# A cross-attention kernel: its first rows on two DMA queues, its key weights split later on ScalarE

## The chip, the cores and the metric

The program runs on one core of a Trainium2 chip. The metric is the time of one execution in device microseconds (us). The engines are TensorE (PE, with its weight loads PEld), VectorE (DVE), ScalarE (ACT), GpSimd (POOL) and SyncE (SP). SP and ACT also issue the DMAs, each on a queue of its own.

## The reference

One row block `x` of 256 tokens by 512 reads a context of 25088 tokens by 512. Three blocks follow one another: cross-attention with a sigmoid instead of a softmax, causal attention with latents, and a layer of eight experts of which each token takes one. The change touches only what stands at the start of the first:

```
def ref_xattn(q, ctx):                       # q = layernorm(x)
    qp = q @ Wq.T + bq                       # 256 x 128
    kp = ctx @ Wk.T + bk                     # 25088 x 128
    vp = ctx @ Wv.T + bv
    z = sigmoid(qp @ kp.T / sqrt(128))
    return z @ vp
x = x + ref_xattn(layernorm(x), ctx_1024)
x = x + attn(layernorm(x)); x = x + ffn(layernorm(x))
```

## The kernel before

Products that need more precision than one pass gives are made of three: each operand is split into a rounded "high" part (a Copy on ACT) and a "low" part (a subtraction on DVE), and high x high, high x low and low x high are summed in PSUM. The context goes by in 49 tiles of 512 tokens. For each tile `b` the kernel computes its keys (L336), the scores against the queries (L354), the sigmoid (L364) and the sum of weights times context rows (L395). The value projection is applied once, after the loop. A context tile comes in twice, turned (`rawt`, split into `th`, `tl`) and plain (`rawn`, split into `nh`, `nl`), in halves of 512 KB.

No scheduler decides the order. `put` appends an operation to a list of its engine, with the semaphores that it waits for, and each engine plays its list in the order in which the program wrote it. An engine that waits holds up all that stands behind it on its list. DMAs are issued in the same way, as an entry on the list of SP ("sync") or of ACT ("scalar").

The head of the program does this:

- L189 loads the two halves of `x` (128 rows each, 256 KB) into `x_s`, both on SP's queue. Then SP issues the two halves of the first turned context tile (`rawt`), the query weights (`zf`), and more of the context. ACT's queue has the key weights `wk_s` (256 KB, L190), the identity matrix `id_s` (64 KB, used to transpose) and the biases `bqk_s` (1 KB).
- L267 lets PE multiply zeros (`wz`) 22 times, so that it works while the first data are on their way.
- L272 runs a Sqrt on one element, which loads that table early. L273 writes `wkh`, the high part of the key weights.
- L281 and L282 (DVE) take mean and variance of each half of `x`, the first half and then the second. L283, called the root here, takes the square root on ACT. L284 to L289 make the reciprocal deviation of it on DVE with one Newton step. L296 writes the normalised rows `h_s`, and L299 transposes them on PE into PSUM.
- L304 runs a Sigmoid on one element of ACT, for which the table of the main loop is loaded. Behind it ACT splits the turned context (`th`, L230), copies the transposed rows to `hT` (L318), and goes on with `nh`, `qph` and `kph`.
- L292 (`first_keys`) is the keys of tile 0, in an order of its own: high parts of the first two chunks, their product with `wkl` (the low part of the key weights, L307 on DVE), and so on. L322 is the queries. Then come the first scores, L354.

```
root = put("scalar", lambda e: e.activation(stat(18), mv[:, :, 1], ACT.Sqrt, bias=eps_s[:]), [m, EPS0], "lnq")
...
put("scalar", lambda e: e.activation(sq[0:1, 6:7], sq[0:1, 0:1], ACT.Sigmoid), [SQ0], "sgw")
low_t = [split_t(0, k) for k in range(2)]
```

Of the kernel before, what the change touches and what calls it, by code (L numbers as in the profile page):

```python
# [6 lines left out]
ACT = mybir.ActivationFunctionType  # L7
# [13 lines left out]
class Queues:  # L21
# [8 lines left out]
    def put(self, eng, fn, waits=(), sig=None, inc=1):  # L30
        for m in waits:
            sem, value = m
            if self.seen.get((eng, sem), 0) < value:
                self.seen[(eng, sem)] = value
                self.lists[eng].append(("wait", self.sems[sem], value))
        if sig is None:
            self.lists[eng].append(("do", fn, None, 0))
            return None
        if sig not in self.sems:
            self.sems[sig] = self.ctx.enter_context(self.nc.semaphore("s_" + sig))  # L40
            self.count[sig] = 0
        self.count[sig] += inc
        self.lists[eng].append(("do", fn, self.sems[sig], inc))
        return sig, self.count[sig]

    def dma(self, eng, dst, src, sig, waits=()):
        return self.put(eng, lambda e: e.dma_start(dst, src), waits, sig, 16)
# [11 lines left out]
def program(nc, x, ctxn, ctxt, wkt, wqt, wvt, bqk, bv, kvd, kup, vup, wq, qrope, krope, wo, gate, wg, wu, wd,  # L59
# [3 lines left out]
    with ExitStack() as ctx:  # L63
        q = Queues(nc, ctx)
        put, dma = q.put, q.dma

        def sb(name, shape, dt=F32):
            return ctx.enter_context(nc.sbuf_tensor(name, shape, dt))
# [11 lines left out]
        def bank(i):  # L80
            return ps[i // 2][:, 512 * (i % 2):512 * (i % 2) + 512]
# [4 lines left out]
        x_s = sb("x_s", [P, 2, D])  # L86
# [42 lines left out]
        def sm(name, shape, dt=F32):  # L129
            return stream.enter_context(nc.sbuf_tensor(name, shape, dt))  # L130
# [12 lines left out]
        wk_s = sm("wk_s", [P, 512])  # L143
        wkh = sm("wkh", [P, 512], F32R)
# [41 lines left out]

        xr = x.rearrange("a (r p) d -> p (a r) d", p=P)

        DX = [dma("sync", x_s[:, r, :], xr[:, r, :], f"dx{r}") for r in range(2)]  # L189
        DWK = dma("scalar", wk_s[:], wkt, "dwk")  # L190
        DID = dma("scalar", id_s[:], ident, "did")
        wq0 = zf
# [20 lines left out]
        def load_n(b, k):  # L213
            old = [] if b == 0 else hm if (b, k) == (1, 1) else n_rd[0, 1] if (b, k) == (2, 1) else n_rd[b - 1, k]
            n_ld[b, k] = dma("sync", raw_n(b, k), ctn[b][:, HALF[k]], "dn1b" if (b, k) == (1, 1) else f"dn{k}", old)
# [11 lines left out]
        def split_t(b, k):  # L227
            n = HALF[k]
            free = [] if b == 0 else [KW[k], Tl[0, k]] if b == 1 else [KP[b - 1]]
            Th[b, k] = put("scalar", lambda e: e.activation(th[:, n], raw_t(b)[:, n], ACT.Copy), [t_ld[b, k], *free], "th")  # L230
            return lambda: split_tl(b, k)
# [31 lines left out]
            return low if later else low()  # L263

        WZ = put("gpsimd", lambda e: e.memset(wz[:], 0.0), (), "wz")
        for k in range(22):
            put("tensor", lambda e: e.matmul(bank(7), wz[:, 0:P], wz[:], start=True, stop=True), [WZ])  # L267
        Z0 = put("gpsimd", lambda e: e.memset(zacc[:], 0.0), (), "pz")
        ONE = put("gpsimd", lambda e: e.memset(one_s[:], 1.0), (), "pz")
        EPS0 = put("vector", lambda e: e.memset(eps_s[:], EPS), (), "eps")  # L270
        SQ0 = put("vector", lambda e: e.memset(sq[:], 1.0), (), "sq0")
        WARM = [put("scalar", lambda e: e.activation(sq[0:1, 1:2], sq[0:1, 0:1], ACT.Sqrt), [SQ0], "lnw")]  # L272
        WKH = put("scalar", lambda e: e.activation(wkh[:], wk_s[:], ACT.Copy), [DWK], "wkh")  # L273

        def stat(k, n=2):
            return st[:, k:k + n]
# [3 lines left out]
        for r in range(2):  # L280
            m = put("vector", lambda e, r=r: e.bn_stats(st[:, 6 * r:6 * r + 6], x_s[:, r, :]), [DX[r]], "ln")  # L281
            m = put("vector", lambda e, r=r: e.bn_aggr(mv[:, r, :], st[:, 6 * r:6 * r + 6]), [m], "ln")  # L282
# [7 lines left out]
        def first_keys(w, t, c, wait, opens=False, mark=None):  # L290
            n = slice(512 * c, 512 * c + 512)
            return put("tensor", lambda e: e.matmul(bank(0), w[:, c * P:(c + 1) * P], t[:, n], start=opens,  # L292
                                                    stop=mark == "kp"), wait, mark)

        def first_rows(r):
            h = put("vector", lambda e: e.tensor_scalar(h_s[:, r, :], x_s[:, r, :], mv[:, r, 0:1], stat(26 + r, 1),  # L296
                                                        ALU.subtract, ALU.mult), [m], "lnh")
            for k in range(4):
                f = put("tensor", lambda e, k=k: e.transpose(bank(6 + r)[:, k * P:(k + 1) * P],  # L299
                                                             h_s[:, r, k * P:(k + 1) * P], id_s[:]),  # L300
                        [h, DID], "lnt" if k == 3 else None)
            return f

        put("scalar", lambda e: e.activation(sq[0:1, 6:7], sq[0:1, 0:1], ACT.Sigmoid), [SQ0], "sgw")  # L304
        low_t = [split_t(0, k) for k in range(2)]
        hm = [first_rows(r) for r in range(2)]
        WK = put("vector", lambda e: e.tensor_tensor(wkl[:], wk_s[:], wkh[:], ALU.subtract), [WKH], "wkl")  # L307
        load_n(1, 1)
        low_t[0]()
        for k in range(2):  # L310
            for c in (2 * k, 2 * k + 1):
                first_keys(wkh, th, c, [WKH, Th[0, k]], opens=c == 0)
            for c in (2 * k, 2 * k + 1):
# [17 lines left out]
        def keys(b, turns=None):  # L331
            for i, c in turns or [(i, c) for i in range(3) for c in range(4)]:
                w, t = [(wkh, th), (wkl, th), (wkh, tl)][i]
                old = [KPL[b - 2]] if b >= 2 and i == 0 else []
                wait = old + [WKH, WK, Tl[b, c // 2] if i == 2 else Th[b, c // 2]]
                KP[b] = put("tensor", lambda e, w=w, t=t, c=c, i=i: e.matmul(  # L336
# [347 lines left out]
        f = add()  # L684
# [91 lines left out]
        def a_sums(qt):  # L776
            m = put("vector", lambda e: e.reciprocal(einv[:, qt, :], esum[:, qt, :]),
                    [EX[p, u] for p in range(NU) if units[p][0] == qt for u in range(2)], "rc")
            return put("vector", lambda e: e.tensor_copy(
                eexp, einv[:, qt, :].rearrange("p (h o) -> p h o", o=1).to_broadcast([P, 16, 32])),  # L780
                [m] + ([RR[0]] if qt else []), "rc")

        def a_spread(qt, bk, wait):
            for t in range(4):
                f = put("tensor", lambda e, t=t: e.matmul(
                    bank(bk)[:, P * t:P * t + P], eexp[:, 4 * t:4 * t + 4, :].rearrange("p h o -> p (h o)"), id_s[:],
                    start=(t == 0), stop=(t == 3)), wait, "rr" if t == 3 else None)
            return f
# [68 lines left out]
        f = a_sums(0)  # L857
# [20 lines left out]
        f = a_sums(1)  # L878
# [4 lines left out]
        f = a_spread(1, 4, [f, EX[4, 0]])  # L883
# [221 lines left out]
```

How the kernel before makes its waits and increments, by code:

```python
    def play(self, eng, e):  # L49
        for item in self.lists[eng]:
            if item[0] == "wait":
                e.wait_ge(item[1], item[2])
            else:
                ins = item[1](e)
                if item[2] is not None:
                    ins.then_inc(item[2], item[3])
```

## Time and profile before

| | us |
|---|---|
| median of 3 runs | 577.13 (576.76 to 577.57) |
| the profiled execution | 577.08 |
| its span, from first to last instruction | 575.3 |
| outside the span | 1.8 |
| PE busy | 569.4 |
| DVE busy | 456.4 |
| ACT busy | 401.7 |

The span begins when the first engine works. What the profile calls idle is time before an instruction in which its engine had nothing to do, with the releaser behind the arrow.

### The profile page before, as it was taken

What the parts mean: (1) busy time and instruction counts of PE and PEld (TensorE: products, weight loads), DVE (VectorE), ACT (ScalarE), POOL (GpSimd) and SP (SyncE); (2) the same over time, 40 slices, a digit from 0 to 9 for tenths busy, and PEclk for the clock granted to TensorE, in tenths of its full rate; (3) what the DMA queues carried; (4) which work ended last, traced back from release to release, by engine and by line L of the source; (5) the groups of instructions that cost most, each with busy time, mean ns of one, the idle gap of its engine ahead of it and who ended that gap; (6) DMA issues with size and microseconds to landing.
All of it is one profiled execution on the core that took longest, in us unless ns stands there. A gap on an engine that the chain in (4) does not pass through costs nothing.

```text
span 575.3 us, 8075 instructions
## 1 busy us (share of the span) xinstructions
PE 569.4 (99%) x3010; PEld 477.2 (83%) x3010; DVE 456.4 (79%) x494; ACT 401.7 (70%) x542; POOL 1.7 (0%) x7
## 2 busy tenths in 40 slices
PE   8999999999999999999999999999999999999998
PEld 5888888888888888888888888888888887877887
DVE  6987878787878797889787978787878798887742
ACT  6776767676768687768667877776776784797321
POOL 1000000000000000000000000000000000000000
DMA  8668777768677877777778877767787743000201
GB/s 327 229 199 248 233 237 236 225 221 240 218 220 251 265 244 238 236 255 259 226 246 254 254 227 250 219 221 222 217 275 234 229 142 114 33 1 2 74 1 38
DMA packets 33239, 115.90 MB, mean 201 GB/s; under 512 B 4080, under 2 KB 4784, under 8 KB 32944
## 3 DMA queue, kind: packets, MB, share of 16 engines
q1 hardware_dynamic: 32768, 115.05, 62.7%
q8 instruction: 24, 0.39, 0.3%
q10 hardware_dynamic: 432, 0.33, 0.2%
q14 instruction: 15, 0.12, 0.1%
HBM read 114.84 MB, written 0.52 MB: 201 GB/s over the span
## 4 chain that ended last, share of the span: by engine, by line
PE 92%; ACT 3%; DMA 2%; DVE 2%; issue 1%; DVEq 0%; ACTq 0%; SPq 0%
PE ps L395 44%; PE ps L336 22%; PE ps L354 12%; PE ps L924 4%; PE ps L956 2%; DMA rawn<-in_ctxn 1%; PE ps L813 1%; PE ps L525 1%; ACT w L742 1%; PE ps L722 1%; PE ps L657 1%; PE ps L749 1%; PE ps L606 1%; DMA x_s<-in_x 1%; PE ps L292 1%
## 5 line engine op out<-in xcount | busy, mean ns | idle before, releaser
L395 PE MATMUL ps<-nh,zl 128*128 128x512 f32 x388 | 142.8, 390 | 0.1
L395 PE MATMUL ps<-nh,zh 128*128 128x512 f32 x388 | 142.7, 390 | 0.0
L395 PE MATMUL ps<-nl,zh 128*128 128x512 f32 x388 | 142.5, 389 | 0.0
L369 DVE TENSOR_TENSOR zl<-zf,zh 128x1024 fp32r<-128x1024 f32 x49 | 60.1, 1226 | 79.6 <-ACT zh L368 79.6
L255 DVE TENSOR_TENSOR nl<-rawn,nh 128x1024 fp32r<-128x1024 f32 x96 | 114.0, 1221 | 1.4 <-issue 0.8
L235 DVE TENSOR_TENSOR tl<-rawt,th 128x1024 fp32r<-128x1024 f32 x96 | 113.2, 1218 | 1.8 <-ACT th L230 1.7
L252 ACT ACTIVATE nh<-rawn 128x1024 fp32r<-128x1024 f32 x96 | 99.8, 1057 | 12.3 <-DMA rawn<-in_ctxn 11.1
L230 ACT ACTIVATE th<-rawt 128x1024 fp32r<-128x1024 f32 x96 | 96.3, 1053 | 2.3 <-DMA rawt<-in_ctxt 2.3
L364 ACT ACTIVATE zf<-ps 128x512 f32<-128x512 f32 x98 | 58.2, 597 | 56.3 <-PE ps L354 50.6
L395 PEld LDWEIGHTS ps<-nh,zl 128*128 128x128 f32 x388 | 72.7, 188 | 16.0 <-DVE zl L369 1.0
L395 PEld LDWEIGHTS ps<-nl,zh 128*128 128x128 f32 x388 | 72.9, 188 | 15.2
L395 PEld LDWEIGHTS ps<-nh,zh 128*128 128x128 f32 x388 | 72.5, 188 | 15.5 <-ACT zh L368 0.5
L341 ACT ACTIVATE kph<-ps,bqk_s 128x512 fp32r<-128x512 f32 x49 | 33.8, 690 | 47.8 <-PE ps L336 47.7
L372 DVE TENSOR_TENSOR zacc<-zacc,zf 128x1024 f32<-128x1024 f32 x49 | 59.8, 1220 | 0.0
L354 PE MATMUL ps<-qph,kpl 128*128 128x256 f32 x196 | 55.0, 283 | 0.0
L354 PE MATMUL ps<-qpl,kph 128*128 128x256 f32 x196 | 55.0, 283 | 0.0
L354 PE MATMUL ps<-qph,kph 128*128 128x256 f32 x196 | 54.8, 282 | 0.0
L368 ACT ACTIVATE zh<-zf 128x1024 fp32r<-128x1024 f32 x49 | 52.1, 1063 | 1.6
L336 PE MATMUL ps<-th,wkh 128*128 128x512 f32 x192 | 52.6, 394 | 0.0
L336 PE MATMUL ps<-th,wkl 128*128 128x512 f32 x192 | 51.7, 390 | 0.0
L336 PE MATMUL ps<-tl,wkh 128*128 128x512 f32 x192 | 51.6, 390 | 0.0
L336 PEld LDWEIGHTS ps<-th,wkl 128*128 128x128 f32 x192 | 36.1, 188 | 8.1
(193 smaller groups left out, 618.5 us busy)
## 6 DMA issues: line engine op xcount, KB each, us to landing
rawn<-in_ctxn SPq DMA_DIRECT2D x97, 512.0 KB, 6.4
rawt<-in_ctxt SPq DMA_DIRECT2D x96, 512.0 KB, 4.8
h_s<-in_wg SPq DMA_DIRECT2D x4, 512.0 KB, 6.7
h_s<-in_wu SPq DMA_DIRECT2D x4, 512.0 KB, 6.6
wds<-in_wd SPq DMA_DIRECT2D x4, 512.0 KB, 3.9
raw<-in_ctxt SPq DMA_DIRECT2D x2, 512.0 KB, 8.7
h_s<-in_wvt SPq DMA_DIRECT2D x2, 512.0 KB, 7.6
wq_s<-in_wq SPq DMA_DIRECT2D x1, 1024.0 KB, 10.1
```

The costliest lines, as they stand in the source:

```text
L230: Th[b, k] = put("scalar", lambda e: e.activation(th[:, n], raw_t(b)[:, n], ACT.Copy), [t_ld[b, k], *free], "th")
L235: Tl[b, k] = put("vector", lambda e: e.tensor_tensor(tl[:, n], raw_t(b)[:, n], th[:, n], ALU.subtract), [t_ld[b, k], Th[b, k]] + ([KL[k]] ...
L252: Nh[b, k] = put("scalar", lambda e: e.activation(hi, raw_n(b, k), ACT.Copy), [n_ld[b, k]] + free, "nh")
L255: Nl[b, k] = put("vector", lambda e: e.tensor_tensor(lo, raw_n(b, k), hi, ALU.subtract), [n_ld[b, k], Nh[b, k]] + free, "nl")
L336: KP[b] = put("tensor", lambda e, w=w, t=t, c=c, i=i: e.matmul(bank(b % 2), w[:, c * P:(c + 1) * P], t[:, c * 512:(c + 1) * 512], start=(i ...
L341: KPH[b] = put("scalar", lambda e: e.activation(kph[:], bank(b % 2), ACT.Identity, bias=bqk_s[:, 1:2]), [KP[b], DBK] + ([S[b - 1]] if b el ...
L354: m = put("tensor", lambda e, o=o, js=js, k=k, w=w, i=i, j=j: e.matmul(o, k[:, js], w[:], start=(i == 0 and j % 2 == 0), stop=(i == 2 and ...
L364: m = put("scalar", lambda e, g=g, gs=gs: e.activation(zf[:, gs], bank(2 + g), ACT.Sigmoid, scale=SC), [S[b, g]] + ([ZL[b - 1], ZA[b - 1]] ...
L368: ZH[b] = put("scalar", lambda e: e.activation(zh[b % 2][:], zf[:], ACT.Copy), [ZF[b]] + av, "zh")
L369: ZL[b] = put("vector", lambda e: e.tensor_tensor(zl[b % 2][:], zf[:], zh[b % 2][:], ALU.subtract), [ZH[b]] + av, "zl")
L372: ZA[b] = put("vector", lambda e: e.tensor_tensor(zacc[:], zacc[:], zf[:], ALU.add), [ZF[b], Z0] + ([ZA[b - 1]] if b else []), "za")
L395: m = put("tensor", lambda e, z=z, n=n, i=i, j=j, r=r: e.matmul(bank(4 + r), z[:, j * T + r * P:j * T + r * P + P], n, start=(b == 0 and i ...
```

## The change

The first half of `x` is issued on ACT's queue, ahead of the key weights, and the second half stays alone on SP's queue. The split of the key weights (`wkh`) is moved on ACT's list from before the root to behind it, which is ahead of the Sigmoid. The multiplications of zeros go from 22 to 20.

```
-        DX = [dma("sync", x_s[:, r, :], xr[:, r, :], f"dx{r}") for r in range(2)]
+        DX = [dma(("scalar", "sync")[r], x_s[:, r, :], xr[:, r, :], f"dx{r}") for r in range(2)]
         DWK = dma("scalar", wk_s[:], wkt, "dwk")
         DID = dma("scalar", id_s[:], ident, "did")
...
-        for k in range(22):
+        for k in range(20):
             put("tensor", lambda e: e.matmul(bank(7), wz[:, 0:P], wz[:], start=True, stop=True), [WZ])
...
-        WKH = put("scalar", lambda e: e.activation(wkh[:], wk_s[:], ACT.Copy), [DWK], "wkh")
...
+        WKH = put("scalar", lambda e: e.activation(wkh[:], wk_s[:], ACT.Copy), [DWK], "wkh")
         put("scalar", lambda e: e.activation(sq[0:1, 6:7], sq[0:1, 0:1], ACT.Sigmoid), [SQ0], "sgw")
```

ACT's list from the start of the program, of the kernel before (`x_s` is missing here, and L273 is the high part of the key weights, L283 the root):

```order
L47 DMA wk_s<-in_wkt 128x512
L47 DMA id_s<-in_ident 128x128
L47 DMA bqk_s<-in_bqk 128x2
L272 ACT_TABLE_LOAD
L272 ACTIVATE sq<-sq 1x1
L273 ACTIVATE wkh<-wk_s 128x512
L283 ACTIVATE st<-st,eps_s 128x2
L304 ACT_TABLE_LOAD
L304 ACTIVATE sq<-sq 1x1
L230 ACTIVATE th<-rawt 128x1024 x2
```

The same list of the changed kernel, in which L282 is the root and L303 the high part of the key weights:

```order
L47 DMA x_s<-in_x 128x512
L47 DMA wk_s<-in_wkt 128x512
L47 DMA id_s<-in_ident 128x128
L47 DMA bqk_s<-in_bqk 128x2
L272 ACT_TABLE_LOAD
L272 ACTIVATE sq<-sq 1x1
L282 ACTIVATE st<-st,eps_s 128x2
L303 ACTIVATE wkh<-wk_s 128x512
L304 ACT_TABLE_LOAD
L304 ACTIVATE sq<-sq 1x1
L230 ACTIVATE th<-rawt 128x1024 x2
```

One DMA is added at the head of ACT's queue, and `wkh` now stands between the root and the second table load.

SP's list at the same place, as a difference (`x_s` is the rows, `rawt` the turned context, `zf` holds the query weights):

```order
 L1024 UNCONDITIONAL_BRANCH
-L47 DMA x_s<-in_x 128x512 x2
+L47 DMA x_s<-in_x 128x512
 L47 DMA rawt<-in_ctxt 128x1024 x2
 L47 DMA zf<-in_wqt 128x512
```

SP issues one DMA less, so that all behind it moves up by one place; nothing else on SP's list, on DVE's or on PE's moves, but for the two multiplications of zeros.

## Rows read from the trace of the kernel before

**Rows 1.** One stretch: length, busy us (count) of PE, PEld, DVE, ACT, POOL, granted clock, DMA.

```profile
30.00:545.00 515.00, 513.09 (x2727) 433.14 (x2726) 420.55 (x440) 373.09 (x504) 0.00 (x0) 1.00 0.66 208
```

**Rows 2.** Chain that ended last, first 14 us: start, duration, what.

```profile
0.73 3.54 DMA x_s<-in_x
...
7.83 1.11 PE ps L299 x8
...
9.01 2.54 PE ps L292 x10
```

**Rows 3.** Timeline of ACT: start, duration, instruction, count, idle time before.

```profile
4.49 0.63 ACT L273 ACTIVATE wkh<-wk_s 128x512 fp32r<-128x512 f32 x1 [0.86 <-DMA wk_s<-in_wkt]
6.11 0.29 ACT L283 ACTIVATE st<-st,eps_s 128x2 f32<-128x2 f32 x1 [0.99 <-DVE st L282]
6.42 1.28 ACT L304 ACT_TABLE_LOAD   x1
...
7.82 1.99 ACT L230 ACTIVATE th<-rawt 128x1024 fp32r<-128x1024 f32 x2
...
13.78 0.69 ACT L341 ACTIVATE kph<-ps,bqk_s 128x512 fp32r<-128x512 f32 x1
```

**Rows 4.** Timeline of DVE, 4 to 10 us.

```profile
4.30 0.69 DVE L281 BATCH_NORM_STATS2 st<-x_s 128x6 f32<-128x512 f32 x1 [3.41 <-DMA x_s<-in_x]
5.03 0.18 DVE L282 BATCH_NORM_AGGREGATE st<-st 128x2 f32<-128x6 f32 x1
5.16 0.69 DVE L281 BATCH_NORM_STATS2 st<-x_s 128x6 f32<-128x512 f32 x1
...
8.15 0.68 DVE L307 TENSOR_TENSOR wkl<-wk_s,wkh 128x512 fp32r<-128x512 f32 x1
```

**Rows 5.** Timeline of DMA issues on both queues (SPq, ACTq).

```profile
0.73 0.86 SPq L47 DMA_DIRECT2D x_s<-in_x  x2
1.65 0.90 SPq L47 DMA_DIRECT2D rawt<-in_ctxt  x2
1.17 0.46 ACTq L47 DMA_DIRECT2D id_s<-in_ident  x1
```

**Rows 6.** DMAs issued 0.7 to 1.1 and 1.6 to 2.0 us: KB, us to landing.

```profile
wk_s<-in_wkt ACTq DMA_DIRECT2D x1, 256.0 KB, 3.7
x_s<-in_x SPq DMA_DIRECT2D x1, 256.0 KB, 3.5
...
rawt<-in_ctxt SPq DMA_DIRECT2D x1, 512.0 KB, 5.7
id_s<-in_ident ACTq DMA_DIRECT2D x1, 64.0 KB, 4.2
```

**Rows 7.** DMA packets, 2.8 to 3.6 us, then 5.2 to 6.4: packets, MB, share (q1 SP's, q10 ACT's).

```profile
DMA packets 160, 0.33 MB, mean 410 GB/s; under 512 B 0, under 2 KB 0, under 8 KB 160
q1 hardware_dynamic: 80, 0.16, 52.8%
q10 hardware_dynamic: 80, 0.16, 52.5%
...
DMA packets 208, 0.38 MB, mean 315 GB/s; under 512 B 116, under 2 KB 116, under 8 KB 208
```

**Rows 8.** The multiplications of zeros, L267 alone, in two stretches of 3 us: PE, PEld, clock.

```profile
1.30:4.30 3.00, 2.99 (x8) 1.06 (x9) 1.00 0.68 235
4.60:7.60 3.00, 3.00 (x15) 1.25 (x13) 1.00 1.03 378
```

**Rows 9.** Weight loads of PE that waited: idle time before and its releaser.

```profile
7.83 0.88 PEld L299 LDWEIGHTS ps<-id_s,h_s 128*128 128x128 f32 x8 [0.56 <-DVE h_s L296]
8.98 0.30 PEld L292 LDWEIGHTS ps<-th,wkh 128*128 128x128 f32 x2 [0.27 <-issue]
14.52 0.54 PEld L354 LDWEIGHTS ps<-qph,kph 128*128 128x128 f32 x4 [0.29 <-ACT kph L341]
```

**Rows 10.** Timeline of PE around its longest idle time behind the head.

```profile
488.27 0.71 PE L590 MATMUL ps<-id_s,h_s 128*128 128x128 f32 x4 [0.47 <-ACT h_s L586]
```

More of the change, by code:

```diff
@@ L187, in program @@
         xr = x.rearrange("a (r p) d -> p (a r) d", p=P)
-        DX = [dma("sync", x_s[:, r, :], xr[:, r, :], f"dx{r}") for r in range(2)]
+        DX = [dma(("scalar", "sync")[r], x_s[:, r, :], xr[:, r, :], f"dx{r}") for r in range(2)]
         DWK = dma("scalar", wk_s[:], wkt, "dwk")
@@ L265, in program @@
         WZ = put("gpsimd", lambda e: e.memset(wz[:], 0.0), (), "wz")
-        for k in range(22):
+        for k in range(20):
             put("tensor", lambda e: e.matmul(bank(7), wz[:, 0:P], wz[:], start=True, stop=True), [WZ])
@@ L272, in program @@
         WARM = [put("scalar", lambda e: e.activation(sq[0:1, 1:2], sq[0:1, 0:1], ACT.Sqrt), [SQ0], "lnw")]
-        WKH = put("scalar", lambda e: e.activation(wkh[:], wk_s[:], ACT.Copy), [DWK], "wkh")
         def stat(k, n=2):
@@ L302, in first_rows @@
             return f
+        WKH = put("scalar", lambda e: e.activation(wkh[:], wk_s[:], ACT.Copy), [DWK], "wkh")
         put("scalar", lambda e: e.activation(sq[0:1, 6:7], sq[0:1, 0:1], ACT.Sigmoid), [SQ0], "sgw")
```

## The prediction

> **What bounds the kernel now.** I read the stretches first. Between 30 and 545 us TensorE is busy for 513.09 of 515.00 us [rows 1]: the main loop is bound by PE, and it has next to no idle time in which a late start could be made up. So the question is only when PE begins its real work, and whether its chain from there stays as it is. The chain of waits says what sets that start: the first half of `x` (0.73 to 4.27 us), then the statistics and the root, then the 8 transposes at 7.83, and the first keys, L292, at 9.01; from there on the chain lies on PE without a break in the part that I read, the first 60 us [rows 2]. Third, the timelines of ACT and DVE for the same 14 us [rows 3, 4], because the first keys need two things at once: PE free of the transposes (8.94), and the high part `th` of the first context half from ACT. ACT did two halves from 7.82 in 1.99 us; with an overlap of 0.09 the first ended at about 8.87 [rows 3]. PE's weight load came at 8.98 [rows 9]. So the chain names the transposes, but ACT was only about 0.1 us behind them in slack. That is the place at which this change works.
>
> **Part 1, the rows on two queues.** The issue of one DMA takes about 0.43 us, and SP issued the second half of `x` some 0.45 us behind the first [rows 5]. Now both are issued at 0.73. In the kernel before two transfers of the same size were also issued at 0.73, one on each queue: that on SP's landed after 3.5 us, that on ACT's after 3.7 [rows 6]. The chain has the first at 4.27; the wait of `wkh` puts the second at 4.43 to 4.46 [rows 2, 3]. The first half of `x` now takes the later of the two places, and the statistics of that half come first on DVE's list. They began at 4.30 [rows 4], and I expect them at 4.46: +0.16 (bounds 0 and +0.19).
>
> What the earlier landing of the second half gives: its statistics began at 5.16, 0.05 before the aggregate ahead of them ended [rows 4]. Instructions of DVE that don't depend on each other overlap by 0.08 to 0.09 here (two of 0.69 and 0.18 could at best be 0.82 apart instead of 0.86). So at most 0.04 us was waited for the second half, and I take 0.03. The root goes from 6.11 to 6.11 + 0.16 - 0.03 = 6.24 (bounds 6.07 and 6.30).
>
> **Part 2, the high part of the key weights behind the root.** Before, `wkh` (0.63 us) ran at 4.49, inside an idle stretch of ACT: 0.99 us of idle time were left between it and the root, so it cost nothing [rows 3]. Now this cover is gone. Behind the root ACT has no idle time: the table load, the Sigmoid on one element and `th` follow one another. The whole 0.63 us and its gap of 0.02 lie on ACT's way to `th`. With the steps of before between the starts (0.31, 1.29 and 0.11 us): root 6.24, `wkh` 6.55, table load 7.20, Sigmoid 8.49, `th` 8.60 instead of 7.82. The first half of `th` ends at 9.65. ACT's results reach PE 0.05 us later (`kph` ends at 14.47, the waiting weight load starts at 14.52 [rows 3, 9]), the multiplication 0.03 behind that: 9.73 instead of 9.01. **The sum is +0.72 us.** If the first half of `x` lands as early as before, it is +0.56; with the latest root it is +0.78.
>
> Does `wkh` find its data at 6.55? The key weights are issued second on ACT's queue, at 1.17, where `id_s` was [rows 5]. From 2.8 to 3.6 us both queues had transfers with packets of 2 KB in flight, and they moved 80 packets each at 410 GB/s together [rows 7]: packet for packet. The next pair is the key weights (128 packets of 2 KB) and the first half of `rawt` (128 of 4 KB), 0.79 MB, or 1.92 us at 410 GB/s. Added to the landings of the first pair (4.27 and 4.43), that gives 6.2 to 6.35: 0.2 us in time. Against it: from 5.2 to 6.4 us the queues only moved 315 GB/s [rows 7], by which it is 2.5 us and 6.9; and the half of `rawt` itself landed at 1.65 + 5.7 = 7.35 [rows 5, 6]. This is the second rival.
>
> The Trainium skill's page "DMA: Bandwidth & Descriptors", section "Queues, rings and completion order", says that an engine drains some 9 to 17 descriptors of one ring before it switches to the next. Here a transfer has 128 packets over 16 engines, 8 each, so by that rule one transfer would have gone out whole before the other; the equal counts of [rows 7] speak against it. By it the key weights could land earlier than 6.2, and the sum would stay at +0.72, since the root comes later in any case.
>
> **Part 3, two multiplications of zeros less.** The zeros ended at 7.76 before (1.31 + 6.45, the last at 0.21 apart); 15 of them fit in 3 us late in the stretch, 8 early in it [rows 8], which is the step from 1.2 to 2.4 GHz. The list without two ends at 7.33. The transposes don't wait for PE but for `h_s`: their weight load was idle for 0.56 us until DVE released it [rows 9]. They start 0.13 later with the root, at 7.96, and end at 9.07. So PE idles from 7.33 to 7.96 and from 9.07 to 9.70. The removal costs nothing and brings nothing, unless the clock reacts, which is the first rival.
>
> **Part 4, what stands behind.** The low part `wkl` on DVE follows `h_s` (8.15 [rows 4], then 8.28), long after `wkh` ends at 7.18, and is ready before 9.73. The identity matrix is issued third on ACT's queue and pairs with the second half of `rawt`: 0.59 MB behind 6.3 is 7.75, against a need at 7.96; a delay of some tenths there is still hidden by ACT (9.65). SP's transfers are issued 0.45 us earlier, which makes nothing late. After the first keys, `kph`, the scores and the loop depend on PE in the same order, and all shift by the same 0.72.
>
> **The forecast** is made on the profiled execution: 577.08 + 0.72 = 577.80 us. That execution lies 0.05 from the median of the runs, 577.13, which changes nothing. About 0.2%, 1.15 us, is what a measurement of this kernel can tell from no change; so faster means below 575.98 and slower above 578.28.
>
> **The rivals.**
>
> *The clock falls in the new idle time (slower).* PE now works 1.11 us out of the 2.37 between 7.33 and 9.70, the emptiest stretch of the whole trace. If its clock fell to 1.2 GHz there and stayed for the 3.2 us or so that it took to rise at the start (from 1.31 to about 4.5), PE would do half the work in that time: +1.6 on top, 577.8 + 1.6 = 579.4. It decides as soon as the fall comes before about 9.7. Against it: at 488 us PE waited 0.47 us with transposes on either side, and 4 transposes took 0.71 us there, as fast as in the head [rows 10, 2]. 6%. The Trainium skill's page "TensorE: Matmul & The Clock Gate", Part 1, has the clock fall after an idle window; neither gap leaves PE idle for long beside what it did at the start, and no row here shows a fall.
>
> *The key weights land late (a little or clearly slower).* `wkh` waits with all of ACT behind it, at one us for each us beyond 6.55. At 6.9 it is 577.08 + 0.72 + 0.35 = 578.15, at 7.35 it is 577.08 + 0.72 + 0.80 = 578.60. For it: the dip in [rows 7]. Against it: what ran then on ACT's queue were the tiny packets of `bqk_s`, which now come two transfers later. 18%, and somewhat over half of it above 578.28.
>
> *The shift is hidden or the root comes earlier (no change).* The change may do what its first part says, rows that are there sooner. But even a root 0.4 us earlier would leave `wkh` waiting for its data until 6.2 or 6.3, and `th` not before 8.3: +0.45. Only if the key weights were there by then as well, or if PE's chain had slack behind 9 us, would the time stay at 577.1. 10%. For faster than 575.98 I see no mechanism, only what I have overlooked: 4%.
>
> **How the numbers follow.** Forecast 62% (577.8, its own range 577.4 to 578.2 with the bounds above and the scatter of 0.4 us in the runs), late key weights 18% (578.1 to 578.6), clock 6% (579.4), no change 10% (577.1), faster 4%. Slower than 578.28: 6 + 10 = 16%. Faster: 4%. The rest, 80%, is within 0.2%. The range 577.0 to 578.7 leaves out the clock, the gain and the edge of each case.
>
> **What the profile of the changed kernel would show.** Step 1: the first statistics at 4.46, the second 0.82 to 0.86 later, the root at 6.24. Step 2: `wkh` at 6.55 with no wait for its DMA, `th` at 8.60, the first keys at 9.73. Step 3: PE's last zeros end at 7.33, and the first keys are 0.46 to 0.54 apart per pair as before. Step 4: the scores, L354, at 15.24 instead of 14.52, and a span of 576.0. I am wrong if `wkh` waits for its DMA by more than 0.1, if first keys run at half speed, if the transposes wait for the identity matrix, or if the root comes before 6.0.

## The result and the profile after

The changed kernel is slower: a median of 578.72 us (11 runs, 578.41 to 580.39) against 577.26 (11 runs, 576.74 to 578.42), a ratio of 1.0032 with a 95% interval of 1.0023 to 1.0040, which is +1.3 to +2.3 us. The medians lie 1.46 us apart where +0.72 was forecast. The profiled execution took 578.85 with a span of 577.1, so +1.8 in the span against 575.3.

All of it arises in the first 11 us. The stretches of the kernel after (columns as in [rows 1]) show PE as full in the loop as before, and 1.82 us less work in the first 30 us than the 28.55 us that PE did there before:

```profile
0.00:30.00 30.00, 26.73 (x120) 18.78 (x121) 21.24 (x31) 19.98 (x26) 1.66 (x7) 1.00 0.71 257
30.00:545.00 515.00, 513.13 (x2727) 433.44 (x2726) 422.38 (x441) 374.61 (x504) 0.00 (x0) 1.00 0.67 208
```

The chain that ended last no longer begins with `x` [rows 2]. It begins with the key weights:

```profile
1.17 6.57 DMA wk_s<-in_wkt
7.73 0.02 issue
7.76 0.63 ACT wkh L303
...
9.90 0.95 ACT th L230
10.85 0.14 issue
10.99 2.56 PE ps L291 x10
```

The timeline of ACT, against [rows 3]:

```profile
6.53 0.29 ACT L282 ACTIVATE st<-st,eps_s 128x2 f32<-128x2 f32 x1 [2.19 <-DVE st L281]
7.76 0.63 ACT L303 ACTIVATE wkh<-wk_s 128x512 fp32r<-128x512 f32 x1 [0.93 <-DMA wk_s<-in_wkt]
8.40 1.28 ACT L304 ACT_TABLE_LOAD   x1
...
9.81 1.99 ACT L230 ACTIVATE th<-rawt 128x1024 fp32r<-128x1024 f32 x2
```

`th` starts at 9.81 instead of 7.82. Those 1.99 us come apart into the root, 0.42 later (6.53 for 6.11), the 0.64 of `wkh`, and 0.93 of idle time in which ACT waited for the key weights. The first keys start later by the same amount: 10.99 for 9.01, +1.98. The three parts are read along ACT's timeline and are not independent costs: `wkh` starts when its data land, so an earlier root only lengthens the wait. In e11's trace the root came at 6.15, the wait was 1.41, and `wkh` still began at 7.85. About 0.2 of it is regained in the loop: there the trace of before has 0.14 us of idle time of PE between 300 and 480 us that this one doesn't have.

The timeline of DVE, against [rows 4], shows the two statistics:

```profile
4.79 0.69 DVE L280 BATCH_NORM_STATS2 st<-x_s 128x6 f32<-128x512 f32 x1 [3.90 <-DMA x_s<-in_x]
...
5.62 0.66 DVE L280 BATCH_NORM_STATS2 st<-x_s 128x6 f32<-128x512 f32 x1
```

The DMA issues by the time of issue (0.7 to 1.1, 1.1 to 1.6 and 1.6 to 2.0 us), with the us to landing, against [rows 6]:

```profile
x_s<-in_x ACTq DMA_DIRECT2D x1, 256.0 KB, 4.0
x_s<-in_x SPq DMA_DIRECT2D x1, 256.0 KB, 3.9
...
rawt<-in_ctxt SPq DMA_DIRECT2D x1, 512.0 KB, 6.1
...
wk_s<-in_wkt ACTq DMA_DIRECT2D x1, 256.0 KB, 6.6
...
id_s<-in_ident ACTq DMA_DIRECT2D x1, 64.0 KB, 7.4
```

The key weights, issued at 1.17, land at 7.74, 3.3 us later than before. The first half of `rawt`, issued at 1.18, lands at 7.3. The identity matrix lands at about 9.1, and PE's transposes now wait for it: 

```profile
1.31 6.65 PE L267 MATMUL ps<-wz 128*128 128x512 bf16 x20 [1.31 <-POOL wz L265]
9.24 1.07 PE L298 MATMUL ps<-id_s,h_s 128*128 128x128 f32 x8 [1.28 <-DMA id_s<-in_ident]
10.99 0.70 PE L291 MATMUL ps<-th,wkh 128*128 128x512 f32 x2 [0.69 <-ACT th L230]
```

What the queues moved from 4.8 to 6.0 us (packets, MB, share; q1 is SP's, q10 ACT's) shows how the key weights came in:

```profile
DMA packets 97, 0.29 MB, mean 242 GB/s; under 512 B 2, under 2 KB 2, under 8 KB 97
q1 hardware_dynamic: 49, 0.19, 70.7%
q10 hardware_dynamic: 48, 0.10, 27.4%
```

49 packets of `rawt` against 48 of the key weights: they took turns one for one, as in [rows 7], but at 242 GB/s, not 410. From 4.2 to 7.2 us, the whole time in which packets of the key weights were on their way, the queues moved 0.96 MB at 319 GB/s, where the prediction had 0.79 MB at 410.

### The profile page after: what moved, and what is told of

The parts are those of the page before. It is cut to its first block, busy times and chain, and to the rows that moved or that the text cites. A ratio compares the mean times of both kernels' runs of the same rounds, so it can differ in the third digit from the quotient of the medians.

```text
span 577.1 us, 8071 instructions
## 1 busy us (share of the span) xinstructions
PE 569.3 (99%) x3008; PEld 477.3 (83%) x3008; DVE 456.8 (79%) x494; ACT 402.4 (70%) x542; POOL 1.7 (0%) x7
## 4 chain that ended last, share of the span: by engine, by line
PE 95%; ACT 2%; DMA 1%; DVE 1%; issue 0%; ACTq 0%; DVEq 0%
PE ps L395 46%; PE ps L336 23%; PE ps L354 12%; PE ps L924 4%; PE ps L956 2%; DMA wk_s<-in_wkt 1%; PE ps L813 1%; PE ps L525 1%; ACT w L742 1%; PE ps L722 1%; PE ps L657 1%; PE ps L749 1%; PE ps L606 1%; PE ps L291 1%; PE ps L770 1%; PE ps L785 0%
```

## The experiments

Theory A: the loss is a sum of three parts on ACT's way to `th`: the root comes later because the first half of `x` has ACT's place, `wkh` works in the open, and `wkh` waits for key weights that arrive late, since each of their packets waits for one of `rawt`. (The first part counts only as far as `wkh` does not wait for its data.) Theory B, in several forms: the place of `wkh` alone does it, or a slow stretch of the queues at a fixed time, or PE's clock.

All medians stand beside those of the kernel before in the same comparison: 577.14 (e1 to e3), 577.02 (e5 to e8), 577.14 (e10, e11).

### e1: only the move of wkh

On the kernel before:

```
-        WKH = put("scalar", lambda e: e.activation(wkh[:], wk_s[:], ACT.Copy), [DWK], "wkh")
...
+        WKH = put("scalar", lambda e: e.activation(wkh[:], wk_s[:], ACT.Copy), [DWK], "wkh")
         put("scalar", lambda e: e.activation(sq[0:1, 6:7], sq[0:1, 0:1], ACT.Sigmoid), [SQ0], "sgw")
```

> Only the move of wkh behind the root; queues and the 22 multiplications of zeros as in the kernel before. Theory A (the loss of the changed kernel has three parts that add up: root 0.42 later, wkh's own work 0.65, wait for its data 0.92): here only the second is left. The key weights land at 4.4 as before, the root stays at 6.11, wkh starts at 6.42 with no wait, th at 8.47, first keys at 9.65 (+0.6 to +0.65 against 9.01), time +0.6, near 577.9. Theory B (the place of wkh alone does it, whatever its data): first keys at 10.9 and +1.5 to +1.8.

Measured: 577.37 us (11 runs), ratio 1.0001 (0.9992 to 1.0010): +0.23, with an interval of -0.5 to +0.6. The profiled execution was the slowest of the eleven (578.0). Its timeline of ACT:

```profile
6.41 0.29 ACT L282 ACTIVATE st<-st,eps_s 128x2 f32<-128x2 f32 x1 [2.78 <-DVE st L281]
6.62 0.61 ACT L303 ACTIVATE wkh<-wk_s 128x512 fp32r<-128x512 f32 x1
7.25 1.28 ACT L304 ACT_TABLE_LOAD   x1
```

With its data there, `wkh` starts 0.21 behind the root, and the table load 0.84 behind it instead of 0.31 [rows 3]: the move costs 0.53 on ACT, not 0.65, since the two instructions overlap by 0.08. Theory B in its first form is refuted: no 1.5 us. That the median rose by 0.23 only is less than A expected; e3 and e9 bear on it.

### e2: only the queues

The changed kernel with `wkh` back ahead of the root (behind L272) and 22 multiplications of zeros.

> Only the queues are changed; wkh stays ahead of the root, 22 multiplications of zeros. Theory A: the key weights land at 7.7 as in the changed kernel, wkh ends at 8.4 and holds up the root until then: root 8.4, h_s at 9.5, transposes at 10.1, first keys at 11.2, that is 0.2 to 0.3 later than in the changed kernel (10.99), time +2.0 to +2.2. Theory B: with wkh back at its place the time is that of the kernel before, within 0.3.

Measured: 578.85 (7 runs, one of them 580.68 at a lower clock), ratio 1.0035 (1.0024 to 1.0047). Timeline of ACT:

```profile
7.80 0.63 ACT L273 ACTIVATE wkh<-wk_s 128x512 fp32r<-128x512 f32 x1 [3.55 <-DMA wk_s<-in_wkt]
8.34 0.28 ACT L283 ACTIVATE st<-st,eps_s 128x2 f32<-128x2 f32 x1
```

The key weights landed at 7.8 again, and now hold the root too. The first keys started at 11.22, 0.23 later than in the changed kernel, as A said; the time is +1.71, below the +2.0 to +2.2 that A expected. So the queues alone make the loss. With them changed, `wkh` behind the root is 0.23 better in the traces; the times of the two kernels can't be told apart. The first half of `x` landed after 3.9 us here.

### e3: only the multiplications of zeros

```
-        for k in range(22):
+        for k in range(20):
```

> Only two multiplications of zeros less. Both theories: the zeros end 0.43 earlier, the transposes still wait for h_s, first keys at 9.01, time within 0.2 of the kernel before. A rival by the clock: PE stays or falls at half speed in the idle time, then the first keys are 0.43 apart instead of 0.23, and +1 us or more.

Measured: 576.79 (11 runs, 576.66 to 577.11), ratio 0.9994 (0.9985 to 1.0003). The interval reaches 1, so a gain is not proven, but the runs are much closer together than those of before (576.72 to 578.79). First keys at 9.09, 0.23 apart, no sign of a lower clock.

### e9: the kernel before once more

> The kernel before once more, for the scatter of its landings: the first half of x at 4.3 to 4.6, the key weights at 4.4 to 4.8, the first keys at 9.0 to 9.4.

Measured: 577.27 in one execution, the first half of `x` after 3.7 us, the key weights after 3.9. The timeline of PE shows what e3 takes away:

```profile
1.31 7.64 PE L267 MATMUL ps<-wz 128*128 128x512 bf16 x22 [1.31 <-POOL wz L265]
8.79 1.04 PE L299 MATMUL ps<-id_s,h_s 128*128 128x128 f32 x8
9.58 0.70 PE L292 MATMUL ps<-th,wkh 128*128 128x512 f32 x2
```

The same 22 multiplications ended at 7.76 in the trace of before and at 8.95 here, because PE's clock rose later: between 4.3 and 5.3 us 6 of them started in before and 4 here, and the next us again 6 and 4. (The granted clock says 1.00 in both stretches of [rows 8], so that this rise is read from the counts alone.) The transposes waited for them, not for `h_s`, and the first keys came at 9.58, outside the 9.0 to 9.4 that I expected. In such an execution a later `th` would be partly hidden. In e1's trace the zeros ended late too, at 8.73, with the transposes at 8.57, but there `th` still came last: the first keys waited 0.23 us for it and began at 9.84, +0.83. Why the median of e1 rose by 0.23 only is therefore not shown.

### e4: the changed kernel once more

> The changed kernel once more, for one more trace of it: how much do the landings scatter? If the late landings are a property of the order, the first half of x lands near 4.8, the key weights near 7.7 and the identity matrix near 9.1, each within 0.2, and the rate of the DMA queues falls to 200 to 250 GB/s between 5.0 and 6.0 us again. If they are chance, they differ by more than 0.5.

Measured: 580.08. The landings are a property of the order: the first half of `x` after 4.1 us, the key weights at 7.56, the identity matrix at 9.1; 215 and 256 GB/s in the two stretches from 4.8 and 5.4 us. But this execution took 1.2 us more than the profiled one, and PE's timeline shows where:

```profile
9.18 1.07 PE L298 MATMUL ps<-id_s,h_s 128*128 128x128 f32 x8 [1.81 <-DMA id_s<-in_ident]
10.82 0.74 PE L291 MATMUL ps<-th,wkh 128*128 128x512 f32 x2 [0.58 <-ACT th L230]
11.35 1.05 PE L291 MATMUL ps<-th,wkl 128*128 128x512 f32 x2
12.21 1.05 PE L291 MATMUL ps<-th,wkh 128*128 128x512 f32 x2
```

From 11.35 the pairs are 0.85 apart instead of 0.46: PE ran at 1.2 GHz (granted clock 0.50 from 11.4 to 14.7) until nearly 15 us. The fall came not in the idle time but 0.5 us behind the start of the first keys. The queries, L322, began 3.95 us behind the first keys instead of 2.39: 1.56 us lost. PE had been idle for 1.81 and 0.58 us on either side of the transposes. Two of the 11 runs of the changed kernel have the same time and granted clock over the whole run (580.39 and 580.35, 0.997), and none of the 66 runs of e1, e3, e5, e6, e7 and e10.

### e5: the key weights on SP's queue

On e2's kernel:

```
-        DWK = dma("scalar", wk_s[:], wkt, "dwk")
+        DWK = dma("sync", wk_s[:], wkt, "dwk")
```

> The first half of x on ACT's queue as in the changed kernel, but the key weights on SP's queue behind the second half and ahead of rawt; wkh ahead of the root, 22 multiplications of zeros. Theory A (the key weights were late since each of their packets of 2 KB took turns with one of 4 KB of rawt): now they take turns with the packets of the identity matrix (512 B) and land at 5.1 to 5.4; wkh is done by 6.1 and hides again ahead of the root. What is left is the later landing of the first half of x on ACT's queue (+0.3 to +0.5): first keys at 9.3 to 9.6, time +0.3 to +0.5. Theory B (the queues are slow between 4.8 and 6 us whatever stands in them): the key weights land at 6.3 or later and hold the root up.

Measured: 577.12 (11 runs), ratio 0.9999 (0.9991 to 1.0008). Timeline of ACT:

```profile
5.20 0.63 ACT L273 ACTIVATE wkh<-wk_s 128x512 fp32r<-128x512 f32 x1 [1.56 <-DMA wk_s<-in_wkt]
6.24 0.29 ACT L283 ACTIVATE st<-st,eps_s 128x2 f32<-128x2 f32 x1 [0.41 <-DVE st L282]
```

With the packets of the identity matrix as partners the key weights land at 5.2, 2.5 us sooner than in the changed kernel, while `rawt` waits. `wkh` is hidden again, and the whole loss is gone, with the first half of `x` still on ACT's queue. Its landing after 3.7 us, against 3.5 of the second half on SP's, puts the root at 6.24: +0.13, as in the working of the prediction, and not the 0.3 to 0.5 that I expected here. That is agreement within the scatter: with both halves on SP's queue the root came at 6.11 (before), 6.19 (e3), 6.30 (e9) and 6.41 (e1).

### e6: wkh behind the Sigmoid

On the changed kernel:

```
-        WKH = put("scalar", lambda e: e.activation(wkh[:], wk_s[:], ACT.Copy), [DWK], "wkh")
         put("scalar", lambda e: e.activation(sq[0:1, 6:7], sq[0:1, 0:1], ACT.Sigmoid), [SQ0], "sgw")
+        WKH = put("scalar", lambda e: e.activation(wkh[:], wk_s[:], ACT.Copy), [DWK], "wkh")
```

> The changed kernel with wkh behind the Sigmoid, so that ACT loads its table while it would wait for the key weights. Theory A: the wait of 0.92 goes, the 0.65 of wkh's work and the later root stay: root 6.53, th near 9.0, first keys 10.2 to 10.4 (the transposes, which wait for the identity matrix until 9.2, end at 10.3), time +1.2 to +1.3, that is 0.6 to 0.8 less than the changed kernel. If something else than the wait for the key weights makes the loss, the time stays at that of the changed kernel.

Measured: 577.73 (11 runs), ratio 1.0009 (1.0000 to 1.0018): +0.71, 0.75 less than the changed kernel's +1.46. Timeline of ACT:

```profile
7.92 0.61 ACT L304 ACTIVATE wkh<-wk_s 128x512 fp32r<-128x512 f32 x1
8.44 1.99 ACT L230 ACTIVATE th<-rawt 128x1024 fp32r<-128x1024 f32 x2
```

The queues are those of the changed kernel, the data are as late (6.5 us after the issue), but ACT loads its table meanwhile and the wait is gone. The time is less than the +1.2 to +1.3 that I expected, and `th` starts 0.56 sooner than the 9.0 expected: the root came at 6.21 in this execution, not at 6.53. First keys at 10.20: now they wait for the transposes, which had to wait for the identity matrix until 9.38.

### e7: the query weights ahead of rawt

On the changed kernel:

```
+        DWQ = dma("sync", wq0[:, 0:512], wqt, "dwq")
         for k in range(2):
             load_t(0, k)
-        DWQ = dma("sync", wq0[:, 0:512], wqt, "dwq")
```

> The changed kernel with the query weights (packets of 2 KB) ahead of both halves of rawt on SP's queue. Theory A: the key weights now take turns with packets of their own size, and land by 6.0; wkh starts right behind the root (6.5, 6.84) with no wait; the first half of rawt lands near 8, before th wants it at 8.9. First keys at 10.0, time +1.0. Theory B (a slow stretch of the queues tied to the time since the start): the key weights still land at 7 or later, and the time stays at +1.5 or more.

Measured: 577.47 (11 runs), ratio 1.0008 (0.9999 to 1.0016): +0.45, where I expected +1.0; the interval reaches 1. The issues of 1.1 to 1.6 us in this kernel, and then the timelines of ACT and PE:

```profile
wk_s<-in_wkt ACTq DMA_DIRECT2D x1, 256.0 KB, 4.6
zf<-in_wqt SPq DMA_DIRECT2D x1, 256.0 KB, 4.4
```

```profile
6.20 0.30 ACT L282 ACTIVATE st<-st,eps_s 128x2 f32<-128x2 f32 x1 [2.09 <-DVE st L281]
6.41 0.61 ACT L303 ACTIVATE wkh<-wk_s 128x512 fp32r<-128x512 f32 x1
7.04 1.28 ACT L304 ACT_TABLE_LOAD   x1
...
9.62 0.70 PE L291 MATMUL ps<-th,wkh 128*128 128x512 f32 x2 [0.56 <-ACT th L230]
```

With partners of their own size the key weights land at 5.8. `wkh` doesn't wait; its cost is again 0.53. The first keys at 9.62, +0.61, are what the prediction's sum should have been about: root +0.09, `wkh` +0.53.

### e12: rawn ahead of rawt too

On e7's kernel, `load_n(0, 0)` is moved ahead of the two `load_t`.

> As the run with the query weights ahead, and the first half of rawn ahead of rawt too: which transfer is slow? In all traces so far the queues fell to 200 to 300 GB/s for over a microsecond about 0.6 us after the first packets of rawt. If it is the first transfer of 4 KB packets from the context, whichever it is, the dip stays at 5.4 to 6.6 us with rawn; if it belongs to rawt, it comes 1.2 us later. The first keys are late here by 1 us or so, because rawt is.

Measured: 580.09 in one execution, with PE at the lower clock after 1.34 and 1.27 us of idle time. The queues moved from 4.8 to 6.0 us, and then from 6.6 to 8.4:

```profile
DMA packets 215, 0.49 MB, mean 412 GB/s; under 512 B 27, under 2 KB 60, under 8 KB 215
...
DMA packets 254, 0.49 MB, mean 273 GB/s; under 512 B 107, under 2 KB 138, under 8 KB 254
```

In the first stretch they move `rawn`, whose packets also have 4 KB, at full rate. The dip comes with `rawt`, 1.2 us later than in e7. It follows the start of `rawt` in the others as well: in the kernel before its first packets start near 4.7 us and the low rate (283 GB/s) lies between 5.4 and 6.3, in the changed kernel they start near 3.6, and it (260 GB/s) lies between 4.6 and 6.2. It doesn't need the small packets of `bqk_s`: in the changed kernel these start behind 7 us. In the kernel before and in e12 they lie in the dip as well, and may have a share in it there. Why the first reads of `rawt` are slow is open; no run changed how it lies in memory.

### e8: all three transfers cut in two

Each of `x`'s halves and the key weights goes by 64 partitions on each queue, on the kernel before (the lines for `x`; the key weights go in the same way):

```
+        for r in range(2):
+            a = dma("scalar", x_s[LO, r, :], xr[LO, r, :], f"dxa{r}")
+            b = dma("sync", x_s[HI, r, :], xr[HI, r, :], f"dxb{r}")
```

> Each half of x and the key weights are cut in two by partitions, one part on each queue, in the order first half, second half, key weights; wkh ahead of the root, 22 multiplications of zeros. By turns of packets the first half of x shares the engines with nothing else: it lands at 3.9 to 4.0 instead of 4.3, the key weights at 5.1 to 5.3. The root comes at 5.8 to 5.9 (wkh ends about then), the first keys at 8.8 (limited by the zeros, 7.76), time -0.2. If the start of the queues and not the sharing sets the first landing, the first half lands at 4.3 or later, and nothing is won.

Measured: 580.70 (6 runs, three of them at the lower clock), ratio 1.0054 (1.0036 to 1.0073). A clear miss. Timeline of DVE, then of ACT:

```profile
3.92 0.69 DVE L286 BATCH_NORM_STATS2 st<-x_s 128x6 f32<-128x512 f32 x1 [3.03 <-DMA x_s<-in_x]
...
5.67 0.69 DVE L286 BATCH_NORM_STATS2 st<-x_s 128x6 f32<-128x512 f32 x1 [0.84 <-DMA x_s<-in_x]
```

```profile
9.49 1.06 ACT L235 ACTIVATE th<-rawt 128x1024 fp32r<-128x1024 f32 x1 [0.98 <-DMA rawt<-in_ctxt]
```

The first half of `x` did come at 3.9. But the second came at 5.7: the queues moved 133 to 161 GB/s between 3.0 and 4.2 us, with transfers of 64 partitions in both. All that follows is late, `rawt` most. Two more issues on ACT's queue, one more on SP's, and a low rate of such halves are all in it; the run doesn't separate them. PE waited 2.21 us ahead of the transposes in this trace (until 10.94), and its clock stayed up: the first keys ran 0.23 apart.

### e10: the identity matrix first

On the kernel before, with 20 multiplications of zeros:

```
+        DID = dma("scalar", id_s[:], ident, "did")
         DWK = dma("scalar", wk_s[:], wkt, "dwk")
-        DID = dma("scalar", id_s[:], ident, "did")
```

> The kernel before with the identity matrix ahead of the key weights on ACT's queue, and 20 multiplications of zeros; both halves of x stay on SP's queue. If transfers on the two queues go packet for packet, the first half of x now takes turns with packets of 512 B instead of 2 KB and lands at 3.9 to 4.0 instead of 4.3, the second half takes turns with the key weights, which land at 4.8 to 5.0. wkh hides ahead of the root (5.7 to 5.8), the first keys start at 8.6 to 8.7, and the time is 0.3 less than before. If not, all lands as before and the time is within 0.1 of that of the run with 20 multiplications of zeros alone.

Measured: 576.97 (11 runs), ratio 0.9995 (0.9986 to 1.0004). Timeline of DVE, then of ACT:

```profile
3.68 0.69 DVE L281 BATCH_NORM_STATS2 st<-x_s 128x6 f32<-128x512 f32 x1 [2.79 <-DMA x_s<-in_x]
```

```profile
5.79 0.29 ACT L283 ACTIVATE st<-st,eps_s 128x2 f32<-128x2 f32 x1
...
7.73 1.06 ACT L230 ACTIVATE th<-rawt 128x1024 fp32r<-128x1024 f32 x1
9.05 1.06 ACT L230 ACTIVATE th<-rawt 128x1024 fp32r<-128x1024 f32 x1 [0.27 <-DMA rawt<-in_ctxt]
```

The partner decides again: beside packets of 512 B the first half of `x` landed after 2.9 us, 0.6 sooner than beside the key weights. The root came at 5.79. But `th` came at 7.73 only, since now `rawt` is the last to arrive, and the first keys at 8.93 are 0.08 sooner than before. The gain of 0.3 that I expected is turned into a wait for `rawt`: the time is -0.17, beside -0.35 in e3 with the same 20 multiplications, and neither is told from no change.

### e11: 12 multiplications of zeros

The changed kernel with `range(12)` for `range(20)`.

> The changed kernel with 12 instead of 20 multiplications of zeros, which makes PE's idle time ahead of the transposes 1.7 to 3 us longer. If the executions of the changed kernel that took 1.5 us and more beyond the others are those in which PE's clock fell in that idle time, it now falls in most or all executions: first keys 0.43 apart instead of 0.23, about +1.6 on the changed kernel, near 580.3. If they come from something else, the time is that of the changed kernel, 578.7.

Measured: 580.19 (4 runs, 579.75 to 580.68, all at the lower clock), ratio 1.0053 (1.0037 to 1.0069). PE's timeline:

```profile
9.34 1.26 PE L298 MATMUL ps<-id_s,h_s 128*128 128x128 f32 x8 [2.73 <-DMA id_s<-in_ident]
11.09 1.19 PE L291 MATMUL ps<-th,wkh 128*128 128x512 f32 x2 [0.48 <-ACT th L230]
12.08 1.05 PE L291 MATMUL ps<-th,wkl 128*128 128x512 f32 x2
```

The transposes began at the full rate, and from 10.1 to 13.5 us the granted clock was 0.50. All four executions have 0.994 to 0.997 over the whole run, so the clock fell in each, with 2.73 us of idle time ahead of the transposes in the one that has a trace. The price is the same +1.5 (580.19 beside 578.72). The twelve multiplications of zeros took 5.30 us, 0.43 apart throughout, so in this run PE did nothing at the full rate ahead of the gap, besides having a longer gap, and the run doesn't separate the two.

## Why the prediction was wrong

**The direction and the place were right, the size was not.** The prediction put the damage on ACT's way to `th`, and there it was. Of its sum of +0.72 each term can now be held against a measurement.

**The landing of the key weights is the step that failed.** "That gives 6.2 to 6.35: 0.2 us in time" was 7.74 (7.56 and 7.80 in e4 and e2), which alone cost 0.93 us of waiting. The turns of packets were read rightly: 49 against 48. What was wrong is first the rate, 319 GB/s over the whole transfer for 410, then the amount, 0.96 MB for 0.79, and some 0.3 us by which the pair ahead, the two halves of `x`, landed later (4.6 and 4.7 for 4.3 and 4.4). I worked with 410 GB/s although [rows 7] showed 315 for the next stretch, and laid that dip to the tiny packets of `bqk_s`. The changed kernel has the dip without them, and e12 shows that it belongs to `rawt`, the very partner that the change gives to the key weights. The row was in hand, and the half of `rawt` had landed at 7.35 [rows 5, 6]: a transfer that goes packet for packet with it can't be done much before it. The second rival said exactly this, with 578.60 for a landing at 7.35. It deserved to be the forecast, not 18%. e5, e6 and e7 confirm it from three sides: other partners take the wait away (+0.10 and +0.45 in time), other work in the wait halves the loss (+0.71). How the delay divides between the size of the partner's packets and the slow start of `rawt` is not shown: no run pairs the key weights with packets of 4 KB at the full rate.

**`wkh`'s own work** was put at 0.65. Where its data are there it is 0.53 (e1, e7), as it overlaps the root; where it waits for data it is 0.64.

**The root** was put at +0.13, and was +0.42 in the profiled execution. ACT's place landed 0.1 to 0.2 later than SP's in every trace that has this order (4.0 and 3.9, 3.9 and 3.8, 4.1 and 3.9, and 3.7 and 3.5 in e5, e6, e7 and e11), which is the step as told. The rest is scatter: SP's first transfer took 3.5, 3.9, 3.6 and 3.7 us in before, e1, e3 and e9. It doesn't matter to the changed kernel, whose `th` hangs on the key weights, not on the root.

**The zeros** were put at nothing, because they ended before `h_s` was ready. That was one execution: in e9 they ended at 8.95 and held up the transposes. Two less are worth a little (-0.35 in e3, not proven), and cost nothing where PE's gaps are short.

**The clock** was a rival with 6% and +1.6. The price was right (1.56 in e4). The fall came at 11.35 in e4, behind the start of the first keys, and not in the gap. The chance was too small because the gap was: I had 0.63 us ahead of the transposes, and it was 1.28 to 1.81, since they waited for the identity matrix, which landed at 9.1. "7.75, against a need at 7.96" fails for the same rate. The Trainium skill's page "TensorE: Matmul & The Clock Gate", Part 1, ties the fall to an idle window; the traces with a fall (e4, e11, e12) do have idle time ahead of it. But the length of a gap doesn't settle it: the trace of e8 has 2.21 us and those of e2, e6 and the changed kernel 1.86, 1.31 and 1.28 us ahead of the transposes, without a fall. The three with a fall have a second gap behind the transposes (0.58, 0.48 and 1.27 us), as the changed kernel's trace also has (0.69).

**The turns of packets.** "DMA: Bandwidth & Descriptors", section "Queues, rings and completion order", in the Trainium skill has some 9 to 17 descriptors drained before a switch. The changed kernel's 49 and 48 packets within 1.2 us, with 8 of a transfer on each engine, and the landings in e5, e7 and e10 that follow the size of the partner's packets, speak for a switch after each one. The traces don't say which DMA engine a packet ran on, so a block of several on one engine is not excluded by a count.

## What to carry to other kernels

When two queues are busy, a small transfer is delayed by the packets that it takes turns with: pair it with transfers of small packets, or put it on the same queue ahead of the large ones, and bound its landing by that of its partner in the trace, not by bytes over the best rate. A conversion that sat in idle time should not be moved to a chain that has none; if it must wait for data, put it behind work that doesn't need them, such as a table load. Start-up gaps of TensorE of over a microsecond may cost another 1.5 us by the clock in some executions (2 of 11 of the changed kernel), so fill them, but not beyond the moment at which the data are there.

## What the runs showed of the hardware that I had not expected

- The first transfer of a pair landed after 2.9 us beside packets of 512 B and after 3.5 to 3.9 beside packets of 2 KB (e10; before, e1, e3, e9). The key weights landed 6.4 to 6.7 us after their issue beside packets of 4 KB of `rawt` (e4, the changed kernel, e2, e6, e11), 4.6 and 4.9 beside 2 KB (e7, e12), and 4.0 on SP's queue beside 512 B (e5).
- The queues fell from some 410 to between 200 and 316 GB/s, as a mean over a microsecond, soon after the start of `rawt`, in every trace, and not with `rawn` (412 GB/s, e12), which has packets of the same size.
- Two queues with transfers of 64 partitions moved 133 to 161 GB/s for 1.2 us (e8).
- TensorE's clock rose at different times in two executions of one kernel: the same 22 multiplications took 6.45 us (before) and 7.64 (e9). In e2 and e1, which have the same 22, they took 6.87 and 7.42.
